# The second attention walks its edges as one stream of equal steps, with a window of 128 nodes per step and the sums of all tiles in SBUF

## The reference

```python
def _gat_forward(x, W, att_src, att_dst, bias, edge_index):
    loop = jnp.arange(n)                       # every node also sends to itself
    src = concat([edge_index[0], loop]); dst = concat([edge_index[1], loop])
    h = (x @ W).reshape(n, HEADS, OUT_C)       # HEADS 4, OUT_C 64
    a_src = einsum('nhc,hc->nh', h, att_src);  a_dst = einsum('nhc,hc->nh', h, att_dst)
    e = leaky(a_src[src] + a_dst[dst], 0.2)
    ex = exp(e - m[dst]);  denom = segment_sum(ex, dst)      # m: maximum of e per dst
    out = segment_sum(ex / denom[dst] * h[src], dst) + bias
    return relu(out)
```

## Time and profile before

| | us |
|---|---|
| median of three executions | 3118.83 |
| their range | 3116.39 to 3142.96 |
| profiled execution, time | 3093.26 |
| its span in the profile | 3091.6 |
| mean granted TensorE clock (share of 2.4 GHz) | 0.792 |
| attention stage in that span | 856 to 2282 |

### The profile page before, as it was taken

One profiled execution on the slowest core, in us unless ns is written; L12 is line 12 of the kernel. 1 busy time (PEld: TensorE's weight loads), 2 busy tenths in 40 slices (PEclk: granted clock), 3 DMA queues, 4 the chain that ended last, 5 costly groups with the idle time before them and its releaser, 6 DMA issues. The chain is left out here.

```text
span 3091.6 us, 56933 instructions
## 1 busy us (share of the span) xinstructions
PE 2175.2 (70%) x13200; PEld 1947.3 (63%) x13201; DVE 1671.9 (54%) x4625; ACT 974.8 (32%) x2742; POOL 1524.8 (49%) x1476
## 2 busy tenths in 40 slices
PE   5432329994747776776667667666675999999997
PEld 3332318994536665655555556555564999998997
DVE  4554525665835554554345445444456676676664
ACT  2222317773511111111111111111122665565653
POOL 1356644442046665665546555555512455555544
PEclk9755659997957777776777777777665999999999
DMA  7212233333533333333323333333253233333322
GB/s 180 72 47 66 69 110 116 106 112 122 168 84 94 92 91 82 92 94 83 85 73 92 87 85 87 85 87 81 74 162 117 41 67 67 66 66 65 67 45 33
DMA packets 193933, 271.38 MB, mean 88 GB/s; under 512 B 73898, under 2 KB 147477, under 8 KB 193745
## 3 DMA queue, kind: packets, MB, share of 16 engines
q0 software_dynamic: 83248, 203.73, 25.4%
q1 hardware_dynamic: 109865, 66.28, 7.9%
q10 hardware_dynamic: 776, 0.89, 0.1%
HBM read 202.82 MB, written 69.72 MB: 88 GB/s over the span
## 5 line engine op out<-in xcount | busy, mean ns | idle before, releaser
L2070 POOL DMA_INDIRECT at_G<-h_as,at_idx x850 | 809.3, 952 | 712.5 <-issue 443.6
L2274 PE MATMUL at_pAgg<-at_G,at_OH 128*128 128x260 f32 x1700 | 578.6, 514 | 156.1 <-DVE at_ACC L2122 103.4
L2274 PEld LDWEIGHTS at_pAgg<-at_G,at_OH 128*128 128x128 f32 x1700 | 441.6, 267 | 258.3 <-DVE at_G L2104 122.1
L2214 ACT ACTIVATE at_OT<-at_pTr 128x384 f32<-128x384 f32 (+1 forms) x300 | 128.2, 471 | 927.3 <-remote 552.4
L2267 PE MATMUL at_pAd<-at_cur,at_OT 128*128 128x8 f32 x1700 | 280.6, 302 | 158.8 <-ACT at_OT L2214 147.9
L2267 PEld LDWEIGHTS at_pAd<-at_cur,at_OT 128*128 128x128 f32 x1700 | 277.5, 255 | 171.5 <-ACT at_OT L2214 158.5
L1731 ACT ACTIVATE e_full<-e_pH,g_bias_hidden 128x256 f32<-128x256 f32 x640 | 322.7, 504 | 119.6 <-PE e_pH L1614 73.4
L1612 PE MATMUL e_pH<-e_xT_high,e_WA_high 128*128 128x256 f32 x1072 | 310.1, 289 | 15.5 <-ACT e_hT_high L1732 11.2
L1492 POOL DMA_INDIRECT out_dram<-e_ob,e_to x108 | 184.5, 1708 | 261.6 <-DVE e_ob L1888 133.5
L2104 DVE TENSOR_TENSOR at_G<-at_G,at_pIds 128x1536 f32<-128x1536 f32 x150 | 249.8, 1665 | 115.2 <-ACT at_pIds L2221 83.7
L1614 PE MATMUL e_pH<-e_xT_high,e_WA_low 128*128 128x256 f32 x1072 | 301.0, 281 | 0.0
(11 more groups left out here) (357 smaller groups left out, 4261.5 us busy)
## 6 DMA issues: line engine op xcount, KB each, us to landing
e_xs<-slot_rows SPq DMA_DIRECT2D x54, 257.0 KB
at_G<-h_as,at_idx POOLq DMA_INDIRECT x850
b_rows<-expert_out SPq DMA_DIRECT2D x14, 896.0 KB, 6.9
g_raw_first<-in_L_ffn_W_dram POOLq DMA_DIRECT2D x8, 1024.0 KB, 7.9
g_raw_last<-in_L_ffn_W_dram POOLq DMA_DIRECT2D x8, 1024.0 KB
gate_rows<-b_Y SPq DMA_DIRECT2D x7, 924.0 KB, 4.2
xt_ar<-a_og SPq DMA_DIRECT2D x7, 910.0 KB, 4.3
h_as<-b_og SPq DMA_DIRECT2D x7, 910.0 KB, 4.2
```

Of the source, the lines that this page charges most:

```text
L2070: gp.indirect_dma_start(G[j][:, c, :], None, K.T1, bass.IndirectOffsetOnAxis(ap=idx[j][:, c:c + 1], axis=0)).then_inc(gathered[j], 16)
L2274: last = nc.tensor.matmul(pAgg[:, 0:DIM + 4], OH[j][:, c, :], G[j][:, c, :], start=(j == 0 and c == 0), stop=(j == NJ - 1 and c == CHUNKS[ ...
```

## The change

- A step is 15 chunks, `CHUNKS = (5, 5, 5)`, 1920 edges. The steps no longer follow the tiles: step s = 1 to 52 takes edges 1920 (s - 1) onwards, step 0 the last 160 edges (2 chunks, `REST`). 53 steps, 782 gathers.
- `EdgeRanges` takes the lowest and the highest destination of each step ([53 x 60] tables in the place of [98 x 1563]), and makes per step: number of windows of 128 nodes, base node (`K.BASE`), the tile in which it begins, the shift against that tile (`K.SHIFT`), and which tiles are complete after it. The GpSimd iota goes. The tables are broadcast to all partitions. `halves` is replaced by `fill`, `load` and `ranges`, `spans` and `table` are new.
- b0: the output goes straight to its place in `K.NUM` [128, 50, 264], which stays for the attention, so `free` and its wait go. SP loads all edge indices at once (`K.ESRC`, `K.EDST`, four DMAs, rows of 60 B) behind the second `load_results`.
- Attention, own term: one DVE product over [128 x 12544] in `K.NUM` (and one copy of the exponentials) before the loop, in place of 49 loads (L2031) and 49 times L2177 and L2180. `cur`: the terms `adm` are stored to DRAM (`K.ADM`) and SP loads 128 x 32 B per window.
- `G` has two rings (`RINGS = 2`), the messages go to tiles `M[j]` of their own. POOL's gathers of step s + 2 wait for `sources_kept` (a DVE copy of 15 indices after scores 2 of step s) and for the messages of step s.
- Sums: ACT copies `pAgg` to `part`; PE multiplies it in the next window with two one-hot matrices `moves` (made by DVE, 128 x 256) that shift it to its one or two tiles (`pMove`); DVE adds each half to `K.NUM` (`add_part`).
- `settle_tiles` (the eight operations of `finalize`) runs behind the window, for the tiles that are complete.

The core of the diff (cut; the loops around the calls are left out):

```diff
-CHUNKS = (6, 6, 5)
+CHUNKS = (5, 5, 5)
+RINGS = 2
...
-        og = sb("og", [P, 2 * BODY, NC]) if gat_weights else None
+        og = K.NUM if pre == "combine" else sb("og", [P, 2 * BODY, NC]) if gat_weights else None
...
                     load_results(sp, 1)
+                    for to, start in ((K.ESRC, K.SRCP), (K.EDST, K.DSTP)):
+                        sp.dma_start(to[:, 1:STEPS, :], start[0:WHOLE * SE].rearrange("(s p c) -> p s c", p=P, c=ALL)).then_inc(K.edges_in, 16)
+                        sp.dma_start(to[:, 0, 0:REST], start[WHOLE * SE:EDGES + PAD].rearrange("(p c) -> p c", p=P)).then_inc(K.edges_in, 16)
...
             @block.gpsimd
-                        gp.wait_ge(src_kept[j], s + (1 + (DEPTH if j == NJ - 1 else 0)))
-                        freed(gp, agg_done[j], s)
+                def step(s, b):
+                    used = field(gp, s - (RINGS - 1) if isinstance(s, int) else gp.snap(s - (RINGS - 1)), 1, 1, STEPS * TILES)
+                    gp.wait_ge(sources_kept, s - (RINGS - 1))
+                    for j in J:
+                        gp.wait_ge(msg_ready, gp.snap(used * NJ + j))
+                        gather(s, b, j, source[:, b, :])
...
             @block.vector
+                def window(i, b, s, w, again, t):
+                    ch.link(V.tensor_scalar(TI, ids, at, None, ALU.add))
+                    one_hots(s, w, 0)
+                    one_hots(s, w, 1)
+                    scores(ch, i, b, w, 0)
+                    weigh(b, w, 0)
+                    if t is not None:
+                        add_part(w, t, 0)
+                    one_hots(s, w, 2)
+                    scores(ch, i, b, w, 1)
+                    weigh(b, w, 1)
+                    if t is not None:
+                        add_part(w, t, 1)
+                    V.tensor_scalar(moves[:, :], K.iota[:, 0:2 * P], at, None, ALU.is_equal).then_inc(moves_made, 1)
+                    scores(ch, i, b, w, 2)
+                    if not again:
+                        keep_sources(s, b)
+                    weigh(b, w, 2)
+                def step(i, b):
+                        window(i, b, s, w0, False, field(v, previous, 2, 0, TILES - 1))
+                        settle_tiles(previous, w0)
...
             @block.scalar
-                    keep_sources(ahead, 2)
+                    freed(act, agg_done[NJ - 1], w + 1)
+                    nc.scalar.activation(part[:, :], pAgg[:, 0:DIM + 4], ACT.Copy).then_inc(part_kept, 1)
...
             @block.tensor
+                def move(w, half):
+                    if half == 0:
+                        pe.wait_ge(part_kept, w)
+                        pe.wait_ge(moves_made, w)
+                    added_before(pe, w, half)
+                    nc.tensor.matmul(pMove[:, 0:DIM + 4], moves[:, half * P:(half + 1) * P], part[:, :], start=True, stop=True).then_inc(moved, 1)
+                def window(w):
+                    turn(w, 0)
+                    turn(w, 1)
+                    pe.wait_ge(cur_in, w * 16 + 16)
+                    destinations(w, 0, now)
+                    destinations(w, 1, now)
+                    move(w, 0)
+                    aggregate(w, 0)
+                    turn(w, 2)
+                    destinations(w, 2, now)
+                    move(w, 1)
+                    aggregate(w, 1)
+                    aggregate(w, 2)
```

More of the change, by code:

```diff
@@ L343, in __init__ @@
         self.K = K
[L344 to L354, removed]
@@ L419, in spans @@
[L419 to L434 removed]
+        sp.wait_ge(self.step, 8)
@@ new lines, in _ @@
+                sp.dma_start(K.ADM[0:TILES * P, :].rearrange("(t p) k -> p t k", p=P), adm[:, :, :]).then_inc(adm_out, 16)
+                sp.wait_ge(adm_out, 16)
+                with sp.Fori(0, STEPS) as s:
+                    n, w0 = windows(sp, s)
+                    base = field(sp, s, 3, 0, NODES - 1)
+                    with sp.Fori(0, n) as g:
+                        w = sp.snap(w0 + g)
+                        slot = sp.snap(w % DEPTH)
+                        r0 = nc.s_assert_within(sp.snap(base + g * P), 0, TILES * P, skip_runtime_bounds_check_because=
+                                                "a window begins at or under its step's highest destination")
+                        sp.wait_ge(cur_used, w + 1)
@@ L2194, in _ @@
-                v.sem_inc(onehots[NJ - 1], DEPTH)
+                            t = nc.s_assert_within(v.snap(last - n + g), 0, TILES - 1, skip_runtime_bounds_check_because=
+                                                   "a window begins in a tile at or under that of its step's last window")
+                            window(i, b, s, v.snap(w0 + g), True, t)
+                v.sem_inc(cur_used, DEPTH)
                 maxima()
-                V.tensor_scalar(TI, K.iota[:, 0:P], -float(P), None, ALU.add).then_inc(init, 1)
@@ L2197, in _ @@
-                v.wait_ge(init, 1)
                 v.wait_ge(bias_ld, 16)
-                tile(0, 0)
-                with v.Fori(1, TILES) as t:
-                    tile(t, t - 1)
-                n, s0 = tile_steps(v, TILES - 1)
-                s = v.snap(s0 + n)
-                absorb(s)
-                ch = Chain(v, chain, TILES * START + (TILES - 1) * END + s * STEP)
-                finalize(ch, TILES - 1)
+                v.wait_ge(K.edges_in, 64)
+                for b in range(RINGS):
+                    step(0, b)
@@ new lines, in _ @@
+                with v.Fori(1, STEPS // RINGS) as i:
+                    for b in range(RINGS):
+                        step(i, b)
+                for s in range(STEPS // RINGS * RINGS, STEPS):
+                    step(s // RINGS, s % RINGS)
+                n, w0 = windows(v, STEPS - 1)
+                w = v.snap(w0 + n)
+                t = field(v, STEPS - 1, 2, 0, TILES - 1)
+                for half in range(2):
+                    add_part(w, t, half)
+                settle_tiles(STEPS - 1, w)
```

548 lines of the change are left out of this document (268 added, 280 removed).

## The result

The changed kernel took 3486.49 us (median of four, 3480.65 to 3495.88), the kernel before 3130.89 us (median of four, 3116.39 to 3145.52) beside it: ratio 1.1138, 95% interval 1.1066 to 1.1211. It is slower by 11%, 356 us. The forecast was 3560, its range 3080 to 3780, the likeliest case's own 3420 to 3690.

What follows compares the result with a forecast made beforehand. Waits on signals held until 2.2 to 3.1 us behind POOL's gather run were taken to set the pace. 3093.3 + 443 (attention) + 5 (b0) - 5 (a0) = 3536, plus 25.6 = 3562; forecast 3560 us, range 3080 to 3780.

Steps and rivals of the forecast that it cites:

- likeliest case: Attention stage: score signals held until behind each run of 15 gathers, period 35.0 us, total 3560; chance 0.40.
- First score: Start of the attention stage: first score at 886 us, after the own-term product and the first 17 gathers.
- a0 and b0: Two earlier stages: a0 saves DVE operations, -5 us; b0 gains four edge-index DMAs in SP's queue, +5 us.
- Tail: Attention stage after the last score: 22 us before, 27 with the last `moves`, adds and tiles to settle.
- From the run's start to the score: Attention period: 15 gathers without pause 18.5 us, 0.2 to start, 2.5 until held signals are released: 21.2 us.
- From the score to POOL's release: Attention period: 3.15 to aggregate 0, 4.1 for it, 5.3 to score 2, 1.1 to `sources_kept`: 13.65 us.
- the onset: POOL's gather run: signals of other engines still pass early (8.7 us in did), later ones are held.
- rival 3: Attention: `turned`, the signal of the first transposes, is held too; period 38.9 us, total 3760; chance 0.14.
- my 9.0 us: Next window's first transposes due 1.9 + 4.5 + 1.8 + 0.8 = 9.0 us into POOL's run, passing or just not.
- Rival 1: Attention: gathers hide and signals are not held, so no change; period 26.0 us, total 3100; chance 0.10.
- rival 2: Attention: faster, nothing held and TensorE at full clock; period 22.8 us, total 2935; chance 0.18.
- undelayed period: Attention period without any held signal: 13.65 + 1.9 + 4.5 (settling) + 1.8 + 4.1 = 26.0 us; about 21 before the change.

Runs made afterwards that it cites:

- the best variant: Changed kernel with `keep_sources` at the window's start and settling moved between weigh 0 and one-hots 2 of the next window: 2855.4 us, ratio 1.050 to the kernel before.

## Why the prediction was right

**Direction and size.** 3560 was said, 3486 measured, 75 us under the sum of 3562. Of these, 22 are the step from the profiled execution to the median (25.6 us added, 3.5 measured), the rest is the stage; in the profiled executions +443 was said for the stage and +391 measured (its end at 2673.2, said 2725). Of the 52 us between, 50 are in the periods: 51 of 35.0 and one of 27 make 1812, measured 1762. First score: 886 said, 881.7 measured, as the stage's start lay 6 us earlier (a0 and b0 together gave -6, where +5 - 5 was said). Tail 27 said, 29.8 measured.

**One period by its terms.** From the run's start to the score 21.2 said, 1712.55 to 1733.81 = 21.3 measured: 18.5 of issuing, 2.8 behind it. From the score to POOL's release 13.65 said, 1733.81 to 1746.66 = 12.85 measured: to aggregate 0 2.7 (said 3.15), aggregate 0 4.4 (4.1), to score 2 3.9 (5.3: the shift matmul, the add and `moves` lay beside the destination terms and the exponentials and added nothing), scores 2 and the release 1.9 (1.1). The sum held better than its parts; their errors, up to 1.4 us, cancelled to 0.8, which is luck.

**The step that failed in form** is the onset. I took it that signals get through for some 9 us of a run, and that `turned` would then pass or just not. In the changed kernel `turned` of group 1 passes 15.2 us into a run (the copy at 1761.87), while in the period before `ad_ready`, given 13.8 us into its run (1726.34), is held. So no time from the run's start decides; what does is open. That rival 3 did not come about is therefore not to the credit of my 9.0 us. Nor is the release always the run's end: in the last run of the changed kernel the score comes in the middle of it,

```profile
2607.04 4.13 PE L2311 MATMUL at_pAd<-at_cur,g_raw_last 128*128 x20
...
2614.08 0.18 DVE L2119 TENSOR_TENSOR at_Z<-at_G,at_pAd 128x20 f32<-128x20 f32 x1 [8.19 <-remote]
...
2617.45 0.95 POOL L2066 DMA_INDIRECT at_G<-h_as,at_source  x1 [0.30 <-issue]
```

at 2614.08, 4.3 us before the last gather is over, and the period is 27.0. In 50 of 51 it was the end.

**Rival 1 and rival 2 (nothing held).** They were given 2935 to 3100 for the profiled chip, and their condition, that nothing is held, was met on three other chips. On one of them, chip 14, the changed kernel takes 3167 and the kernel before 2722. The other half of rival 2, TensorE at full clock, did not come: 0.68 in that stage. The undelayed period was said to be 26.0 and is 28.2 (mean; 27.0 without the jump back, 31.0 with it): the jump back of DVE's loop, 3.6 us in every second step, was missing in the sum, the settling was right (4.5 said, 4.2 a period gained by its placement). The rivals compared that period with the 28.0 of a chip that holds; they should have put it beside the 21 that the same trace showed for an undelayed step. With that the answer is "slower" on either kind of chip. The size of the forecast, 3560, rested on something that the prediction took for granted without a row for it, that the holding belongs to the kernel: on chips 2, 9 or 14 it would have been some 390 us too high, and that the comparison ran on a chip that holds was luck. The Trainium skill's page "DMA: Bandwidth & Descriptors", section "Rules for kernel authors" (issue early, wait late), agrees with chip 14 as far as the waits go: no score of the changed kernel waits for a gather. It brought no time, since what it hides was not what the period consisted of.

**What isn't settled.** Why some chips hold and others don't, and which instruction of the holding chip's path is blocked. Every execution here was recorded by the profiler, and on the chips that hold its record of updates is full of gaps; whether the recording itself takes part in the holding was not tested. The changed kernel with fewer gathers, with pauses alone, and with settling alone came only onto chips that don't hold, so how much each would win on one that does wasn't seen. And the rest of 130 us between the best variant and the kernel before was not taken apart; no version that beats the kernel before was found.

## What to carry to other kernels

Before costing a change against a mean period, look for the fastest periods in the same trace and ask what the change does to those: a wait that depends on the chip can hide that the new chain is longer. Work that leaves one engine's list and is put between two iterations, where all others stand still, costs its full length, with its value loads and its branch; put it where that engine would wait anyway (here about 4 of the 5.6 us a period that the edit gained). Look at the jump back of a long loop as well: it may cost microseconds, and an edit with another aim may remove it. And compare kernels on the same chip only: the same program took 2722 us on one and 3134 on another.

## What the runs showed of the hardware that I had not expected

- The same kernel differs by 13 to 16% between chips (2709 to 2723 on chips 2, 9 and 14; 3073 to 3134 on 8 and 10), the gathers being issued at the same 0.95 us each, 1.25 apart. Of the 374 us between the two profiled spans of that kernel (3091.6 and 2717.5), 334 lie in the attention stage, where signals between engines are late while POOL issues gathers. On such a chip SP's register instructions slow down as well: 216 of 602 that SP ran between 1000 and 2200 us in the changed kernel took over 0.6 us each, and 155 of 988 in the kernel before; on chip 14 none in either.
- One long DVE operation went with a stop of POOL's issuing. In the first step of the changed kernel:

```profile
859.57 13.23 DVE L2227 TENSOR_TENSOR g_sums<-g_sums,at_exs 128x12544 f32<-128x12544 f32 x1 [0.43 <-ACT at_exs L2283]
859.62 13.99 POOL L2066 DMA_INDIRECT at_G<-h_as,g_edge_src  x1 [0.30 <-issue]
...
873.92 0.94 POOL L2066 DMA_INDIRECT at_G<-h_as,g_edge_src  x1 [0.30 <-issue]
...
881.65 0.17 DVE L2119 TENSOR_TENSOR at_Z<-at_G,at_pAd 128x20 f32<-128x20 f32 x1 [5.33 <-PE at_pAd L2311]
```

The gather that is issued at 859.62 takes 13.99 us, beside the product over [128 x 12544] on DVE (859.57, 13.23 us); its neighbours take 0.95. On chip 14 the 17 gathers of that start have the same mean, 1.72 us (29.2 / 17), and the one issued beside the product (13.23 us) again takes 13.99. It cost nothing here: the first score waited for PE, and not for a gather.
- The jump back at the end of DVE's loop took 3.6 us in the changed kernel, in every second step, on chips of both kinds, and 0.24 us in the kernels with the settling moved.
